# A gated graph network block on one Trainium2 core: first states normalised from a transposed input, with another order of calls

## The chip, the cores and the metric

One core of one Trainium2 chip runs the whole kernel. The metric is the device time in microseconds of that core.

## The reference, cut to what matters

There are 16 graphs of 512 nodes with 128 features each (`x`), and a 512x512 0/1 matrix per graph (`adj`). Two residual layers follow each other.

```
h = relu(layernorm(x))
for i in 0, 1, 2:                        # gated graph network
    m = h @ weight[i];  aggr = A^T @ m
    h = gru(aggr, h)                     # r, z = sigmoid, n = tanh, h = (1-z) n + z h
x = x + h
h = relu(layernorm(x))                   # graph attention, one head
p = h @ W.T;  e = leaky_relu(p@a1 + (p@a2)^T);  mask e where adj == 0
x = x + softmax(e) @ p
```

All values are float32. The normalisations run along the 128 features of a node, with a mean, a variance and eps = 1e-5.

## The kernel before, in words

Nodes of a graph are tiled as C = 4 chunks of P = 128. A "natural" tile has the nodes of a chunk on the partitions and the features along the row (128 x 4 x 128). A "turned" tile has the 128 features on the partitions and the 512 nodes along the row. The GRU works on turned states `hT[s]`; the product with the adjacency takes natural states as weights. A float32 operand of these products is split in a high part (fp32r) and the rest, the low part: `nat_hi`, `nat_lo`, `hT_hi`, `hT_lo`, `agg_hi`, `agg_lo`. A product with a split weight and a split operand is three matmuls of 512 columns (`three`, L1196 to L1198).

**Stages.** Iteration i is a software pipeline over graphs. It does GRU step 0 of graph i, step 1 of graph i-1, step 2 of graph i-2, the second normalisation and projection of graph i-3 (`GA`), and the attention of graph i-4 (`GB`). The steps inside an iteration go 2, 1, 0. Each engine has its own list of calls, written out by hand: `full(i)` for iterations 5 to 15, single lines for the first and the last ones. Waits are on semaphores inside the helpers, so an engine never goes past a call that waits. The order of calls on PE (matmul), DVE, ACT, POOL and the SP queue is therefore the order of the work.

**The first state.** POOL makes from mean and variance (DVE, `x_stats` L693, `x_mean` L702) the scale and the offset of each node: `norm_scale`, L248 to L254, four operations on 128x4. ACT makes `h0 = relu(x*scale + offset)` in natural form (`normed`, L349, four operations of 128x128). PE turns `h0` with four transposes into the PSUM bank `X` (`turn_input`, L1252). ACT copies the bank twice, as `hT[0]` (`first_state`, L362) and as its high part (`first_state_high`, L367). The low part is made on DVE (L742), the natural high part on DVE (`natural_high0`, L728), the natural low part on POOL (`natural_low0`, L260).

**The second normalisation.** DVE makes statistics of `x2` (L815, L822). POOL subtracts the mean (`centre2`, L275), makes the scale (`scale2`, L282 and L284) and multiplies (`normed2`, L291), both on 128x512. PE turns the result (`turn_normed`, L1282), ACT applies relu (`attention_input`, L429), PE projects (`project`, L1298), ACT copies the projection (`values`, L436 and L437).

**The attention.** PE spreads a column over the partitions (`neighbour_terms`, L1306). DVE adds the mask and takes the maximum (`scores`, L838, four of 128x512) and makes the exponents' offsets with four operations of 128x4 (`offsets`, L849, L851, L854, L855). ACT makes two exponentials per chunk (`exps`, L448 and L449), DVE their maximum (`probabilities`, L862). PE turns a chunk (`turn_prob`, L1323), ACT copies it (`turned_prob`, L455), PE multiplies (`attend`, L1338). DVE writes the output (`output`, L881), SP stores it.

**A GRU step.** PE: `neighbours` (L1212, eight matmuls), `from_state` and `from_neighbours` for the banks HN, R, Z and IN. ACT: `neighbours_high` L385, `own_candidate` L395, `reset_gate` L405, `update_gate` L415, `candidate` L423. DVE: `neighbours_low` L754, `reset` L763, `before_tanh` L773, `keep` L781, `renew` L789, `new_state` L799. Then `state_high` (L373 on ACT), `state_low` (POOL L269 or DVE L742), `turn_state` (L1262), `natural_high` (L379) and `natural_low` (L748); the last state goes through `turn_result` (L1273) and `residual` (L807).

**Loads.** The SP queue issues for each graph `x` (256 KB), the adjacency (1024 KB), and later the store. `load_x(i)` waits for `residual` of graph i-4; a ring of four holds the inputs.

Of the kernel before, what the change touches and what calls it, by code (L numbers as in the profile page):

```python
# [27 lines left out]
P = 128  # L28
# [6 lines left out]
def graph_block(nc, x, adj, inner, outer, out):  # L35
# [4 lines left out]
    GA, GB = LAYERS, LAYERS + 1  # L40
    ITERATIONS = B + GB
# [27 lines left out]
    with ExitStack() as ctx:  # L69
# [34 lines left out]
        rstd1 = sb("rstd1", [P, C])  # L104
        mr1 = sb("mr1", [P, C])
        off1 = sb("off1", [P, C])
# [25 lines left out]
        x2c = sb("x2c", [P, C, D])  # L132
        h2n = sb("h2n", [P, C, D])
        h2T = sb("h2T", [P, N])
        hp = sb("hp", [P, RING, C, D + 2])
# [11 lines left out]
        probT = sb("probT", [P, C, C, P])  # L147
# [34 lines left out]
        hT0_done = sem("hT0_done")  # L182

        g_turned, x2_done, st2_done, mv2_done = (sem(n) for n in ("g_turned", "x2_done", "st2_done", "mv2_done"))
        eps2_done, rstd2_done, x2c_done, h2n_done = (sem(n) for n in ("eps2_done", "rstd2_done", "x2c_done", "h2n_done"))
# [9 lines left out]
        def _(sp):  # L195
# [39 lines left out]
        def _(pool):  # L235
# [6 lines left out]
            def norm_scale(i, k):  # L242

                if on(i, 0):
                    pool.wait_ge(mv1_done, (i + 1) * C)
                    if i > 0:
                        pool.wait_ge(h0_done, i * C)
                    pool.tensor_scalar(ve1[:], mv1[:, :, 1], EPS, 0.25, ALU.add, ALU.mult).then_inc(eps1_done, 1)  # L248
                    pool.wait_ge(eps1_done, i + 1)
                    pool.tensor_tensor(rstd1[:], ve1[:], halves[:], ALU.pow).then_inc(rstd1_done, 1)  # L250
                    pool.wait_ge(rstd1_done, i + 1)
                    pool.tensor_tensor(mr1[:], mv1[:, :, 0], rstd1[:], ALU.mult).then_inc(mr1_done, 1)
                    pool.wait_ge(mr1_done, i + 1)
                    pool.tensor_scalar(off1[:], mr1[:], -1.0, None, ALU.mult).then_inc(off1_done, 1)  # L254
# [16 lines left out]
            def centre2(i, k):  # L271

                if on(i, GA) and not last_step(i) and not gru_done(i):
                    pool.wait_ge(mv2_done, (i - (GA - 1)) * C)
                    pool.tensor_tensor(x2c[:], x2[:, i % 3], mv2[:, :, 0:1].broadcast_to([P, C, D]),  # L275
                                       ALU.subtract).then_inc(x2c_done, 1)

# [7 lines left out]

            def normed2(i, k):

                if on(i, GA) and not last_step(i) and not gru_done(i):
                    pool.wait_ge(x2c_done, i - (GA - 1))
                    pool.wait_ge(rstd2_done, i - (GA - 1))  # L290
                    pool.tensor_tensor(h2n[:], x2c[:], rstd2[:].rearrange("p (c o) -> p c o", o=1).broadcast_to([P, C, D]),  # L291
                                       ALU.mult).then_inc(h2n_done, 1)
# [11 lines left out]
            norm_scale(1, 1)  # L304
            norm_scale(2, 2)
            natural_low0(1, 1)
            state_low(1, 1, 2)
            state_low(1, 1, 1)
            natural_low0(2, 2)
            state_low(2, 2, 2)  # L310
            norm_scale(3, 3)
            state_low(2, 2, 1)
            scale2(3, 3)
            natural_low0(3, 3)
            centre2(3, 3)
            normed2(3, 3)
            norm_scale(4, 0)
            state_low(3, 3, 2)
            state_low(3, 3, 1)
            natural_low0(4, 0)  # L320

            for i in range(5, 16):
# [3 lines left out]
            centre2(15, 3)  # L326
            scale2(15, 3)
            normed2(15, 3)
            state_low(15, 3, 1)
            scale2(16, 0)  # L330
            centre2(16, 0)
            normed2(16, 0)
# [1271 lines left out]
```

## Time and profile before

| | |
|---|---|
| median of 3 runs | 466.82 us (466.74 to 468.75) |
| profiled execution, its own time | 466.79 us |
| its span in the profile | 464.9 us |
| granted TensorE clock, mean | 0.999 |
| busy: PE, DVE, ACT, POOL | 97%, 91%, 76%, 32% of the span |
| DMA | 26.42 MB, mean 57 GB/s |

The span is what the engines' records cover, and 1.9 us of the profiled execution's own time lie around it. A busy share is the union of the records of an engine. Records of one engine overlap: a matmul of 512 columns has a record of about 0.39 us, while the next starts 0.23 us after it, and a DVE operation of 0.68 us is followed by the next after 0.60 us. Where work is counted below, it is counted from start to start.

### The profile page before, as it was taken

Reading aid. Unit: us, or ns where it says so; the run is one execution under the profiler, and the core shown is the slowest. Engines: PE = TensorE matmul, PEld = TensorE weight load, DVE = VectorE, ACT = ScalarE, POOL = GpSimd, SP = SyncE. Lnnn points to the kernel's source line nnn. Section 1 sums busy time; section 2 is a strip of 40 time slices with the busy share of each in tenths; the row PEclk is TensorE's granted clock in tenths of the full one; section 3 lists DMA queues with packets and bytes.
Section 4 is the critical chain, followed back from the end, with each engine's and each line's share of the span. In section 5 each row is a group of like instructions: output and inputs, shape, how many; then the busy total and the mean of one; then the engine's idle time right before and its main releaser. Section 6 shows DMA issues by size and latency. Waiting matters only on the chain.

```text
span 464.9 us, 8212 instructions
## 1 busy us (share of the span) xinstructions
PE 451.0 (97%) x2616; PEld 383.0 (82%) x2616; DVE 424.6 (91%) x1101; ACT 351.7 (76%) x636; POOL 147.7 (32%) x165
## 2 busy tenths in 40 slices
PE   8999999999999999999999999999999999998886
PEld 7778778888888888888888888888888888887675
DVE  4979978999999999999999999999999998988986
ACT  3485667878879787877978787896878789595693
POOL 3134163233424224332422423241342324131110
PEclk9999999999999999999999999999999999999999
DMA  8220210200203020020303011030301100000001
GB/s 335 90 90 2 62 52 1 113 10 20 111 24 113 25 113 25 22 93 24 113 25 115 23 35 80 24 115 23 114 23 60 55 25 1 23 2 23 2 23 47
DMA packets 7242, 26.42 MB, mean 57 GB/s; under 512 B 800, under 2 KB 800, under 8 KB 5152
## 3 DMA queue, kind: packets, MB, share of 16 engines
q1 hardware_dynamic: 7200, 25.90, 15.0%
q8 instruction: 22, 0.36, 0.3%
q14 instruction: 20, 0.16, 0.1%
HBM read 21.70 MB, written 4.19 MB: 56 GB/s over the span
## 4 chain that ended last, share of the span: by engine, by line
PE 79%; DVE 6%; issue 5%; ACT 5%; POOL 2%; DMA 1%; POOLq 0%; DVEq 0%; ACTq 0%
PE X L1212 16%; PE G L1338 8%; PE G L1323 5%; PE Z L1196 4%; PE R L1196 4%; PE Z L1198 4%; PE Z L1197 4%; PE R L1198 4%; PE R L1197 4%; PE X L1262 3%; PE G L1298 2%; PE HN L1198 2%; PE HN L1196 2%; PE HN L1197 2%; PE IN L1196 2%
## 5 line engine op out<-in xcount | busy, mean ns | idle before, releaser
L1212 PE MATMUL X<-A_ring,nat_hi 128*128 128x512 f32 x192 | 78.2, 407 | 0.0
L1212 PE MATMUL X<-A_ring,nat_lo 128*128 128x512 f32 x192 | 75.4, 393 | 0.0
L1338 PEld LDWEIGHTS G<-hp,probT 128*128 128x128 f32 x480 | 60.0, 191 | 4.9 <-ACT probT L455 1.8
L1338 PE MATMUL G<-hp,probT 128*128 128x128 f32 x480 | 61.3, 275 | 1.3 <-ACT probT L455 1.3
L405 ACT ACTIVATE tr<-R,bias 128x512 f32<-128x512 f32 x48 | 33.4, 695 | 26.1 <-PE R L1198 25.9
L269 POOL TENSOR_TENSOR hT_lo<-hT,hT_hi 128x512 fp32r<-128x512 f32 x19 | 25.4, 1339 | 79.1 <-ACT hT_hi L373 58.8
L448 ACT ACTIVATE e<-g,nb 128x512 f32<-128x512 f32 x64 | 46.5, 726 | 4.2 <-DVE nb L855 3.0
L455 ACT COPY probT<-G 128x512 f32<-128x512 f32 x60 | 35.5, 592 | 16.8 <-PE G L1323 15.2
L862 DVE SCALAR_TENSOR_TENSOR prob<-e 128x512 f32<-128x512 f32 x64 | 44.6, 699 | 4.0 <-ACT e L449 3.7
L449 ACT ACTIVATE e<-g,nb 128x512 f32<-128x512 f32 x64 | 45.9, 717 | 0.0
L1212 PEld LDWEIGHTS X<-A_ring,nat_hi 128*128 128x128 f32 x192 | 36.0, 188 | 8.5 <-DVE nat_lo L748 0.9
L1212 PEld LDWEIGHTS X<-A_ring,nat_lo 128*128 128x128 f32 x192 | 36.1, 188 | 6.9
L415 ACT ACTIVATE tz<-Z,bias 128x512 f32<-128x512 f32 x48 | 33.0, 688 | 10.4 <-PE Z L1198 10.2
L838 DVE CUSTOM_DVE_ANT_0 g<-G,neg_ring 128x512 f32<-128x512 f32 x60 | 37.8, 687 | 3.3 <-PE G L1306 3.3
L423 ACT ACTIVATE gn<-npre,outer_in 128x512 f32<-128x512 f32 x48 | 35.2, 733 | 4.5 <-DVE npre L773 4.2
L1323 PE MATMUL G<-ident,prob 128*128 128x128 f32 x240 | 36.3, 274 | 1.9 <-DVE prob L862 1.1
L385 ACT CAST agg_hi<-X 128x512 fp32r<-128x512 f32 x48 | 27.9, 581 | 13.5 <-PE X L1212 13.5
L754 DVE TENSOR_TENSOR agg_lo<-X,agg_hi 128x512 fp32r<-128x512 f32 x48 | 32.8, 684 | 5.6 <-ACT agg_hi L385 5.6
L763 DVE SCALAR_TENSOR_TENSOR rv<-tr,hnb 128x512 f32<-128x512 f32 x48 | 33.9, 707 | 2.9 <-ACT tr L405 2.5
L260 POOL TENSOR_TENSOR nat_lo<-h,nat_hi 128x512 fp32r<-128x512 f32 x15 | 20.4, 1357 | 50.6 <-DVE nat_hi L728 50.6
L789 DVE SCALAR_TENSOR_TENSOR fresh<-tz,gn 128x512 f32<-128x512 f32 x48 | 33.0, 687 | 3.6 <-ACT gn L423 1.7
L799 DVE SCALAR_TENSOR_TENSOR hT<-kept,fresh 128x512 f32<-128x512 f32 x48 | 33.1, 690 | 2.6 <-DVE kept L781 0.9
(144 smaller groups left out, 1220.5 us busy)
## 6 DMA issues: line engine op xcount, KB each, us to landing
adj_raw<-in_adj SPq DMA_DIRECT2D x16, 1024.0 KB, 4.9
x_ring<-in_x SPq DMA_DIRECT2D x16, 256.0 KB, 2.7
out_x<-out_sb SPq DMA_DIRECT2D x8, 256.0 KB, 2.0
out_x<-inner_in SPq DMA_DIRECT2D x8, 256.0 KB, 2.0
inner_in<-in_inner SPq DMA_DIRECT2D x1, 384.0 KB, 5.7
outer_in<-in_outer SPq DMA_DIRECT2D x1, 325.0 KB, 5.2
```

The source lines that it names most:

```text
L423: act.activation(gn[:], npre[:], ACT.Tanh, bias=vecs[:, 2:3]).then_inc(gn_done, 1)
L448: act.activation(e1[:, c % 2], g[:, k % 2, c], ACT.Exp, bias=nb1[:, k % 2, c:c + 1])
L449: act.activation(e2[:, c % 2], g[:, k % 2, c], ACT.Exp, bias=nb2[:, k % 2, c:c + 1], scale=SLOPE).then_inc(exp_done, 1)
L455: act.copy(probT[:, c], G1[:]).then_inc(probT_done, 1)
L838: dve.tensor_tensor_reduce(out=g[:, k % 2, c], in0=(HN if gru_done(i - 1) else G0)[:], in1=neg_ring[:, k, c], scale=1.0, scalar=-3.0e38, o ...
L862: dve.scalar_tensor_tensor(out=prob[:, c], in0=e1[:, c % 2], scalar=1.0, in1=e2[:, c % 2], op0=ALU.mult, op1=ALU.max, accum_out=psums[:, k ...
L1196: pe.matmul(acc[:], w_lo, v_hi, start=start, stop=False)
L1197: pe.matmul(acc[:], w_hi, v_lo, start=False, stop=False)
L1198: return pe.matmul(acc[:], w_hi, v_hi, start=False, stop=stop)
L1212: mm = pe.matmul(X[:], part[s][:, c], A_ring[:, (k - s) % RING, c], start=(c == 0 and part is nat_hi), stop=(c == C - 1 and part is nat_lo))
L1323: mm = pe.transpose(own[:, j * P:(j + 1) * P], prob[:, c, j * P:(j + 1) * P], ident[:])
L1338: mm = pe.matmul(own[:, c * D:(c + 1) * D], probT[:, c, j], hp[:, (k + 3) % RING, j, 0:D], start=(j == 0), stop=(j == C - 1))
```

## The change

1. `x` also comes turned from the host, as `xT` (16, 128, 512). For graphs 3 to 15 (`FIRST = 3`) there is no `turn_input` on PE.
2. SP stores scale and offset of such a graph (128 x 8 numbers) to a DRAM scratch and loads them back, spread over all partitions (`norm_rows`, two DMAs, the second waits for the first on the queue), and loads `xT[i]` (`load_xT`).
3. POOL multiplies and adds in place (`scale_turned`, `shift_turned`, two operations of 128x512, whose second input has a step of 8 numbers). ACT makes `hT[0]` and its high part from the result with a relu.
4. The second normalisation becomes one scale and one offset per node: POOL makes them (two more operations of 128x4), ACT applies them (`normed2`, four operations of 128x128). `centre2` and the multiplication on POOL are gone, for all graphs but the last two, where DVE does it as before.
5. `hp` and `probT` have rings of three in place of four. Buffers only, no work.
6. All lists of calls are in another order.

```diff
+            def load_xT(i):
+                if i > FIRST:
+                    sp.wait_ge(hT0_done, i)
+                    sp.wait_ge(hi_done[0], i)
+                sp.dma_start(x_turned[:], xT[i]).then_inc(xT_loaded, 16)
+            def norm_rows(i):
+                sp.wait_ge(off1_done, i + 1)
+                if i > FIRST:
+                    sp.wait_ge(rows_loaded, (i - FIRST) * 16)
+                sp.dma_start(columns[i % 2].rearrange("(p f) -> p f", p=P), norm1[:].rearrange("p a c -> p (a c)")).then_inc(columns_stored, 16)
+                sp.wait_ge(columns_stored, (i - FIRST + 1) * 16)
+                if i > FIRST:
+                    sp.wait_ge(shifted_done, i - FIRST)
+                sp.dma_start(rows[:].rearrange("q p a c -> q (p a c)"), columns[i % 2].partition_broadcast(P)).then_inc(rows_loaded, 16)
...
                 if on(i, 0):
                     load_x(i, i % RING)
                     load_adjacency(i, i % RING)
+                    if i >= FIRST:
+                        norm_rows(i)
+                        load_xT(i)
...
+            def scale_turned(i, k):
+                    pool.tensor_tensor(x_turned..., x_turned..., rows[:, :, 0].rearrange("q p c -> q c p"), ALU.mult).then_inc(scaled_done, 1)
+            def shift_turned(i, k):
+                    pool.wait_ge(scaled_done, i - FIRST + 1)
+                    pool.tensor_tensor(x_turned..., x_turned..., rows[:, :, 1].rearrange("q p c -> q c p"), ALU.add).then_inc(shifted_done, 1)
...
# POOL, full(i)
-                centre2(i - 1, (i - 1) % RING)
+                scale_turned(i - 1, (i - 1) % RING)
+                shift_turned(i - 1, (i - 1) % RING)
+                natural_low0(i - 1, (i - 1) % RING)
                 scale2(i - 1, (i - 1) % RING)
-                normed2(i - 1, (i - 1) % RING)
                 norm_scale(i, i % RING)
                 state_low(i - 1, (i - 1) % RING, 1)
-                natural_low0(i, i % RING)
...
# ACT, full(i), as it is after the change
natural_high(i-1, 2); state_high(i-1, 2); update_gate(i-1, 0); values(i-1); candidate(i-1, 0)
neighbours_high(i, 2); state_high(i-1, 1); normed(i); reset_gate(i, 2); own_candidate(i, 2)
natural_high(i, 1); exps(i, 0); update_gate(i, 2); first_state(i); exps(i, 1)
neighbours_high(i, 1); turned_prob(i, 0); first_state_high(i); own_candidate(i, 1); exps(i, 2)
turned_prob(i, 1); exps(i, 3); reset_gate(i, 1); candidate(i, 2); turned_prob(i, 2)
update_gate(i, 1); neighbours_high(i, 0); normed2(i); candidate(i, 1); turned_prob(i, 3)
reset_gate(i, 0); attention_input(i); own_candidate(i, 0)
# DVE, full(i), as it is after the change
keep(i-1, 0); state_low(i-1, 2); renew(i-1, 0); new_state(i-1, 0); neighbours_low(i, 2)
scores(i); offsets(i); natural_low(i, 1); residual(i); probabilities(i, 0); reset(i, 2)
x2_stats(i); natural_high0(i); probabilities(i, 1); neighbours_low(i, 1); before_tanh(i, 2)
keep(i, 2); state_low(i, 0); probabilities(i, 2); x_stats(i+1); x2_mean(i); adjacency(i)
reset(i, 1); renew(i, 2); probabilities(i, 3); x_mean(i+1); new_state(i, 2); before_tanh(i, 1)
neighbours_low(i, 0); mask(i); keep(i, 1); renew(i, 1); new_state(i, 1); output(i)
reset(i, 0); natural_low(i, 2); before_tanh(i, 0)
# PE, full(i), as it is after the change
neighbours(i, 2); neighbour_terms(i); from_state(2, HN); from_state(2, R); from_neighbours(2, R)
turn_state(i, 1); from_state(2, Z); from_neighbours(2, Z); from_state(1, R); turn_result(i)
from_neighbours(2, IN); neighbours(i, 1); turn_prob(0); from_state(1, HN); from_state(1, Z)
turn_prob(1); attend(0); from_neighbours(1, IN); from_neighbours(1, R); turn_prob(2); attend(1)
from_neighbours(1, Z); from_state(0, R); neighbours(i, 0); attend(2); from_state(0, Z)
turn_prob(3); from_neighbours(0, R); from_state(0, HN); turn_normed(i); attend(3)
turn_state(i, 2); from_neighbours(0, Z); from_neighbours(0, IN); project(i)
```

In iterations 16 and 17 the GRU calls come earlier in the lists of PE, ACT and DVE, ahead of part of the attention of graphs 12 and 13: on PE `from_neighbours(16, 1, R)` and `(16, 1, IN)` now stand ahead of `attend(16, 0)` (the IN one stood behind `attend(16, 3)`), and on DVE `natural_low(16, 2)` now stands ahead of `scores(17)` and `neighbours_low(17, 2)` ahead of `residual(17)`.

## Rows read from the trace of the kernel before

**Rows 1.** Busy time by stretch, one iteration: us, busy PE, PEld, DVE, ACT, POOL, clock, DMA.

```profile
104.10:131.00 26.90, 26.90 (x160) 23.13 (x159) 25.75 (x68) 21.93 (x40) 9.23 (x10) 1.00 0.16 60
```

**Rows 2.** The chain that ended last: `project` of iterations 4 and 11 (start us, us).

```profile
104.35 0.89 PE G L1298 x8
...
292.50 0.89 PE G L1298 x8
```

**Rows 3.** Timeline of PE: a block of four transposes between 512-column matmuls (start, us).

```profile
189.00 0.60 PE L1306 MATMUL G<-ident,hp 128*128 128x128 f32 x4
189.36 0.48 PE L1196 MATMUL HN<-hT_hi,whh_lo 128*128 128x512 f32 x1
189.67 0.39 PE L1197 MATMUL HN<-hT_lo,whh_hi 128*128 128x512 f32 x1
```

**Rows 4.** Groups by line, PE `turn_input`: xcount, busy us, mean ns, idle before.

```profile
L1252 PE MATMUL X<-ident,h 128*128 128x128 f32 x64 | 9.7, 273 | 1.0 <-ACT h L349 0.6 <-DVE agg_lo L754 0.3
```

**Rows 5.** Timeline of PE: `turn_input` of graph 3 and the wait before it.

```profile
67.65 0.63 PE L1252 MATMUL X<-ident,h 128*128 128x128 f32 x4 [0.27 <-DVE agg_lo L754]
```

**Rows 6.** Timeline of ACT in the iteration that begins at 185.68 us.

```profile
185.95 0.48 ACT L436 COPY hp<-G 128x390 f32<-128x390 f32 x1 [0.20 <-PE G L1298]
...
186.49 0.74 ACT L423 ACTIVATE gn<-npre,outer_in 128x512 f32<-128x512 f32 x1
...
189.86 0.61 ACT L373 CAST hT_hi<-hT 128x512 fp32r<-128x512 f32 x1
...
192.87 0.72 ACT L448 ACTIVATE e<-g,nb 128x512 f32<-128x512 f32 x1
...
194.12 0.67 ACT L415 ACTIVATE tz<-Z,bias 128x512 f32<-128x512 f32 x1
194.69 0.71 ACT L448 ACTIVATE e<-g,nb 128x512 f32<-128x512 f32 x1
...
195.91 0.56 ACT L385 CAST agg_hi<-X 128x512 fp32r<-128x512 f32 x1
```

**Rows 7.** Timeline of DVE in the same iteration: `new_state`, first `scores`, first and last of `offsets`.

```profile
188.06 0.69 DVE L799 SCALAR_TENSOR_TENSOR hT<-kept,fresh 128x512 f32<-128x512 f32 x1
...
189.64 0.69 DVE L838 CUSTOM_DVE_ANT_0 g<-G,neg_ring 128x512 f32<-128x512 f32 x1 [0.28 <-PE G L1306]
...
192.21 0.16 DVE L849 TENSOR_TENSOR top<-hp,gmax 128x4 f32<-128x4 f32 x1
...
192.68 0.15 DVE L855 SCALAR_TENSOR_TENSOR nb<-hp,ltop 128x4 f32<-128x4 f32 x1
```

**Rows 8.** Timeline of POOL in the same iteration: `norm_scale` begins and ends, `state_low`.

```profile
185.14 0.19 POOL L248 TENSOR_SCALAR ve<-mv 128x4 f32<-128x4 f32 x1 [6.02 <-DVE mv L702]
...
186.97 0.55 POOL L254 TENSOR_SCALAR off<-mr 128x4 f32<-128x4 f32 x1
190.55 1.30 POOL L269 TENSOR_TENSOR hT_lo<-hT,hT_hi 128x512 fp32r<-128x512 f32 x1 [3.04 <-ACT hT_hi L373]
```

**Rows 9.** DMA issues by line: xcount, KB each, median us to landing.

```profile
x_ring<-in_x SPq DMA_DIRECT2D x16, 256.0 KB, 2.7
```

**Rows 10.** Groups by line, ACT `normed`: xcount, busy us, mean ns, idle before.

```profile
L349 ACT ACTIVATE h<-x_ring,off,rstd 128x128 f32<-128x128 f32 x64 | 26.4, 486 | 7.0 <-POOL off L254 7.0
```

**Rows 11.** Timelines of POOL and DVE: the two places where DVE operations are unusually long.

```profile
42.94 2.20 POOL L260 TENSOR_TENSOR nat_lo<-h,nat_hi 128x512 fp32r<-128x512 f32 x1 [0.37 <-DVE nat_hi L728]
...
43.91 1.78 DVE L763 SCALAR_TENSOR_TENSOR rv<-tr,hnb 128x512 f32<-128x512 f32 x1
...
415.81 1.04 POOL L291 TENSOR_TENSOR h2n<-x2c,rstd 128x512 f32<-128x512 f32 x1
...
415.82 1.57 DVE L862 SCALAR_TENSOR_TENSOR prob<-e 128x512 f32<-128x512 f32 x1 [0.79 <-ACT e L449]
```

**Rows 12.** Timeline of DVE at the end: `new_state` of graph 15, steps 1 and 2.

```profile
423.82 0.69 DVE L799 SCALAR_TENSOR_TENSOR hT<-kept,fresh 128x512 f32<-128x512 f32 x1
...
436.95 0.69 DVE L799 SCALAR_TENSOR_TENSOR hT<-kept,fresh 128x512 f32<-128x512 f32 x1
```

More of the change, by code:

```diff
@@ L40, in graph_block @@
     GA, GB = LAYERS, LAYERS + 1
+    FIRST = 3
     ITERATIONS = B + GB
@@ L319, in _ @@
             state_low(3, 3, 1)
+            scale_turned(4, 0)
+            shift_turned(4, 0)
             natural_low0(4, 0)
-            for i in range(5, 16):
+            scale2(4, 0)
+            norm_scale(5, 1)
+            state_low(4, 0, 1)
+            for i in range(6, 16):
                 full(i)
-            centre2(15, 3)
+            scale_turned(15, 3)
+            shift_turned(15, 3)
+            natural_low0(15, 3)
             scale2(15, 3)
-            normed2(15, 3)
             state_low(15, 3, 1)
             scale2(16, 0)
-            centre2(16, 0)
-            normed2(16, 0)
             state_low(16, 0, 2)
@@ L423, in candidate, with normed2 @@
                     act.activation(gn[:], npre[:], ACT.Tanh, bias=vecs[:, 2:3]).then_inc(gn_done, 1)
+            def normed2(i, k):
+                if on(i, GA) and not last_step(i) and not gru_done(i):
+                    act.wait_ge(off2_done, i - (GA - 1))
+                    for c in range(C):
+                        nd = act.activation(h2n[:, c], x2[:, i % 3, c], ACT.Identity, bias=off2[:, c:c + 1], scale=rstd2[:, c:c + 1])
+                    nd.then_inc(h2n_done, 1)
             def attention_input(i, k):
@@ L551, in _ @@
             reset_gate(3, 3, 1)
+            normed2(3, 3)
             update_gate(3, 3, 1)
@@ L946, in _ @@
             state_high(0, 0, 1)
-            x_mean(2, 2)
             state_low(0, 0, 1)
             natural_low(1, 1, 1)
+            x_stats(2, 2)
+            x_mean(2, 2)
             adjacency(1, 1)
-            adjacency(2, 2)
+            wi_low(1)
             neighbours_low(1, 1, 1)
-            wi_low(1)
+            x_stats(3, 3)
+            mask(2, 2)
             reset(1, 1, 1)
@@ L1055, in _ @@
             reset(4, 0, 0)
-            x_mean(5, 1)
             natural_low(4, 0, 2)
@@ L1108, in _ @@
             probabilities(16, 0, 0)
+            before_tanh(16, 0, 2)
+            probabilities(16, 0, 1)
+            keep(16, 0, 2)
+            neighbours_low(16, 0, 1)
             residual(16, 0)
+            renew(16, 0, 2)
+            probabilities(16, 0, 2)
+            new_state(16, 0, 2)
             x2_stats(16, 0)
-            keep(16, 0, 2)
             x2_mean(16, 0)
-            probabilities(16, 0, 1)
-            probabilities(16, 0, 2)
-            before_tanh(16, 0, 2)
-            neighbours_low(16, 0, 1)
+            reset(16, 0, 1)
             probabilities(16, 0, 3)
-            renew(16, 0, 2)
-            reset(16, 0, 1)
-            new_state(16, 0, 2)
-            output(16, 0)
             before_tanh(16, 0, 1)
@@ L1125, in _ @@
             new_state(16, 0, 1)
+            output(16, 0)
+            natural_low(16, 0, 2)
             scores(17, 1, 0, 4)
             offsets(17, 1, 0, 4)
-            natural_low(16, 0, 2)
+            neighbours_low(17, 1, 2)
             residual(17, 1)
@@ L1132, in _ @@
             probabilities(17, 1, 0)
+            reset(17, 1, 2)
             probabilities(17, 1, 1)
-            neighbours_low(17, 1, 2)
+            before_tanh(17, 1, 2)
             normed2(17, 1)
-            probabilities(17, 1, 2)
-            reset(17, 1, 2)
-            before_tanh(17, 1, 2)
             keep(17, 1, 2)
@@ L1141, in _ @@
             new_state(17, 1, 2)
-            scores(18, 2, 0, 4)
+            probabilities(17, 1, 2)
+            probabilities(17, 1, 3)
             residual(18, 2)
-            offsets(18, 2, 0, 4)
             x2_stats(18, 2)
             x2_mean(18, 2)
-            probabilities(17, 1, 3)
+            scores(18, 2, 0, 4)
+            offsets(18, 2, 0, 4)
+            normed2(18, 2)
             probabilities(18, 2, 0)
-            normed2(18, 2)
             probabilities(18, 2, 1)
@@ L1494, in _ @@
             from_neighbours(4, 0, 0, IN)
-            turn_state(4, 0, 2)
-            for i in range(5, 16):
+            project(4, 0)
+            for i in range(5, 15):
                 full(i)
-            from_state(15, 3, 0, Z)
+            neighbours(15, 3, 2)
+            neighbour_terms(15, 3)
+            from_state(15, 3, 2, HN)
+            from_state(15, 3, 2, R)
+            from_neighbours(15, 3, 2, R)
+            turn_state(15, 3, 1)
+            from_state(15, 3, 2, Z)
+            from_neighbours(15, 3, 2, Z)
@@ new lines, in _ @@
+            from_state(15, 3, 1, R)
+            turn_result(15, 3)
+            from_neighbours(15, 3, 2, IN)
+            neighbours(15, 3, 1)
+            turn_prob(15, 3, 0)
+            from_state(15, 3, 1, HN)
+            from_state(15, 3, 1, Z)
+            turn_prob(15, 3, 1)
+            attend(15, 3, 0)
+            from_neighbours(15, 3, 1, IN)
+            from_neighbours(15, 3, 1, R)
+            turn_prob(15, 3, 2)
+            attend(15, 3, 1)
+            from_neighbours(15, 3, 1, Z)
```

497 lines of the change are left out of this document (262 added, 235 removed).

## The prediction
> **What bounds the kernel now.** First I read the busy time by stretch: in a full iteration PE is busy for all of its 26.90 us, DVE for 25.75, ACT for 21.93 [rows 1]. Then the chain of waits gives the period: `project` starts at 104.35 and, seven iterations on, at 292.50, so one iteration takes 188.15 / 7 = 26.88 us [rows 2]. The timeline of PE shows no gap inside it. So each microsecond taken from PE in the twelve full iterations 4 to 15 is gained, as far as DVE and ACT keep up. Outside them, up to graph 3 and after iteration 15, chains of single operations count as well. I measure the change against the profiled execution, 466.79 us of its own time; the median of the runs, 466.82, is the same number. A difference of 0.5% (2.3 us) is about what a measurement of this kernel can tell from no change.
>
> **PE turns removed.** `turn_input` runs 16 times with four transposes, 64 instructions [rows 4]; 13 of these calls go, 12 of them in the full iterations. The mean of 273 ns is a record's length, not its price. From start to start, a block of four transposes takes 189.36 - 189.00 = 0.36 us, and the first matmul behind it 189.67 - 189.36 = 0.31 us where one matmul behind another takes 0.23, so entering a block costs 0.08 more [rows 3]. Before, `turn_input` stands next to a `turn_prob` and shares that 0.08; but the new list of PE has ten changes of kind per iteration where the old one has eleven. That is 0.36 + 0.08 = 0.44 per iteration. Laying out the new PE list call by call with these prices gives a period of 26.45 us; the same prices laid on the old list give 26.88. Twelve iterations: 12 x 0.43 = 5.2 us. In graph 3 the turn had also waited 0.27 us for `agg_lo` [rows 5], and a wait may stay: between 0.4 and 0.8, I take 0.6.
>
> **The spread by DMA.** `norm_rows` needs scale and offset. `norm_scale` takes 186.97 + 0.55 - 185.14 = 2.4 us [rows 8] and now follows `x_mean`, which the new DVE list places some 18.5 us into the iteration before; behind `scale2` and waits for DVE it ends near 22. Two DMAs in a row follow, and `xT` behind them. No small store and no spread load is in the trace; the nearest row is the load of `x`, 2.7 us for 256 KB [rows 9]. At 2.7 each plus 0.4 to issue, the rows are there 2 us into the iteration, and POOL asks for them no earlier than 5.1, behind `state_low`. The cover is 3 us: the two DMAs may cost 9 in place of 6 before anything moves. Queued behind them on SP are the store, which nothing waits for soon, and `load_x(i+1)`, which waits for `residual` some 8 us into the iteration anyway. Cost nothing; if the cover is gone, `first_state` comes late by the excess.
>
> **POOL.** It loses `centre2` and `normed2` and gains two operations of the same 128x512, 1.04 us each [rows 11], plus two of 128x4. It is busy 9.23 of 26.90 us [rows 1], so this is hidden. What a second input with a step of 8 numbers costs is not in the trace. Between 1.04 us, the row of the same shape, and twice that, I take 1.04, the nearest row, with the other end in the rivals.
>
> **ACT.** `normed2` adds four operations of 128x128: the mean of `normed` is 486 ns [rows 10], some 0.39 from start to start, 1.6 us per iteration, in front of `candidate(i, 1)`. That makes `renew(i, 1)` ready at about 22.1 us in my layout, where DVE, after `mask` and `keep(i, 1)`, arrives at 22.1. So no one waits. `first_state` and `first_state_high` are two ACT operations as before. ACT goes from 21.9 to 23.5 busy of 26.45.
>
> **The second loop.** The new order leaves little slack on one path. After `project` come `values` (0.27 later), `candidate` (0.8 later) [rows 6], `renew`, `new_state` at about n = 2.3, `neighbours_low`, four `scores`, `offsets`. `offsets` ends 192.68 + 0.15 - 188.06 = 4.8 us after `new_state` before [rows 7], of which 0.4 was waiting for `neighbour_terms`, which stands earlier now: 4.4. Then ACT runs without a pause until the third pair of exponentials: three pairs of 1.25 (192.87 to 194.12) and six single operations between 0.47 and 0.57 (194.12 to 194.69) [rows 6], together 6.9, then `probabilities`, 0.8. So `turn_prob(2)` can start at 2.3 + 4.4 + 6.9 + 0.8 = 14.4 to 14.5; PE gets there at 14.5. The two loops are equal, and I give 0.06 per iteration, 0.7 us, for it (bounds 0 and 2).
>
> **Ends.** Until graph 3 the chain is as before: 0, within 1 either way. In the last iterations the GRU of graph 15 is brought forward; its `new_state` started at 423.82 and 436.95 [rows 12]. Laid out by hand, the first comes some 4 us sooner and the second some 2.4, but the attention pushed back has to be done by DVE in the same stretch. Bounds: 1 lost, 3.5 gained; I take 1.5 gained.
>
> Sum: 466.8 - 5.2 - 0.6 + 0.7 - 1.5 = **460.2 us**.
>
> **Rival A: `shift_turned` holds up `offsets`.** This is the one that ends slower. Rows show the mechanism: `reset` took 1.78 us and `probabilities` 1.57 us where they take 0.68 elsewhere, both while a POOL operation of 128x512 ran; the second started 0.01 us after POOL's and got through 0.14 before its end (415.82 + 1.57 - 0.68 = 416.71, against 416.85) [rows 11]. Both read two tiles from SBUF. The Trainium skill (SBUF — State Buffer, "Who interferes with whom") says that a DVE instruction with two SBUF inputs contends with a GpSimd instruction that reads SBUF and that the later one waits for the whole of the other; the two places agree. In the new order, counted from the start of `new_state`: it takes 0.72 with its hand-over, the cast on ACT 0.61, `state_low` 1.30 [rows 6, 8], three hand-overs 0.25, `scale_turned` 1.04, so `shift_turned` runs from 3.93 to 4.97. `offsets` would run from 0.6 + 0.6 + 2.57 = 3.8 to 4.4 [rows 7], and its operations read `hp`, `gmax` and `top`, two SBUF inputs each. If the first slips through and the next is held, the exponentials start 0.66 to 0.86 later, and by the second loop the whole iteration does: 27.1 to 27.3 us against 26.88, so 12 x 0.2 to 12 x 0.4 = 2.6 to 5 us more than before, less 2.1 for graph 3 and the end: 467.3 to 469.7, middle 468.5. It decides from a delay of 0.6 us per iteration on: above that the kernel is slower than before. Against it: two is all that the trace has of DVE held by POOL, no operation of 128x4 among them, and my layout would have to be right to 0.3 us. No run here shows what an operation of four numbers does.
>
> **Rival B: the stepped input is slow on POOL.** At 1.5 us in place of 1.04, `shift_turned` ends about 5.9 after `new_state`, `offsets` is held for 1.6, the period is 28.1, and the sum 466.8 + 12 x 1.2 - 2.1 = 479. For it speaks only that the step is new; for the first value, that POOL's operations here are bound by more than reading, since the same shape takes 1.04 with a broadcast input and 1.30 with an fp32r output [rows 8, 11]. The Trainium skill (Advanced Engine Details and Errata, "SBUF Cachelines") says that accesses which each touch another 16-byte line are penalised; a step of 32 bytes is of this kind, and no run here shows what it costs POOL.
>
> **Rival C: the gain is waited away.** ACT with 23.5 of 26.45 us and DVE with 25.7 have less room, some call comes late by a few tenths, and the period stays near 26.8: 466.8 - 1 - 2.1 = 463.7, between 462 and 466. For it: DVE has only 0.7 us left. Against it: DVE's records overlap, and from start to start it needs about 25.4.
>
> **Rival D: the spread comes late**, so the part does not do what it says and `first_state` waits for a DMA. It needs 9 us for two DMAs. With 10 us it would be 1 late, 0.5 of it felt: 466.8 + 0.6 - 2.1 = 465.3.
>
> **How the numbers follow.** The forecast (PE-bound, 458 to 462) has 0.45, A 0.30, B 0.07, C 0.13, D 0.05. The likeliest is 460.2. The range takes in the forecast, C, D and all of A, and leaves out B and the far ends: 457.5 to 470.5. Faster by over 0.5% (below 464.5): the forecast with its bounds 0.44, most of C 0.08, giving 0.52. Slower (above 469.1): a third of A 0.10, B 0.07, a little of D 0.02, giving 0.19. The rest, 0.29, is within 0.5%.
>
> **What would show it.** Right: `project` every 26.4 to 26.5 us, no wait of PE over 0.1 in the full iterations, no `turn_input` after graph 2, the spread rows landed before POOL's `state_low` ends, the last `new_state` over 2 us nearer to the start than the period alone explains. A: operations of `offsets` with records of 0.8 to 1.0 us in place of 0.16, `turn_prob(2)` waiting for `prob`, a period above 27. B: records of `scale_turned` and `shift_turned` of 1.5 us or more. C: PE waits spread over several lines. D: POOL idle before `scale_turned`, released by a DMA. A period above 26.88 would make the forecast wrong.

## The result: 482.6 us in place of 466.6

The changed kernel takes 482.62 us (median of 6 runs, 482.41 to 484.22), the kernel before 466.63 (6 runs, 464.89 to 468.75). The ratio is 1.0348, with a 95% interval of 1.0322 to 1.0374: slower by 3.5%. The forecast was 460.2, its range ended at 470.5.

The profiled execution of the changed kernel has a span of 482.4 us, that of the kernel before 464.9. It is the slowest of the six (484.22 us); the spans therefore differ by 17.5 us where the medians differ by 16.0. To see where the 17.5 us arose, cut both spans at the start of `neighbours(4, 2)` and of `neighbours(16, 2)` on the timeline of PE (before: 77.93 and 401.42; after: 78.21 and 418.50). Twelve iterations lie between the cuts.

| part of the span | before | after | difference | forecast |
|---|---|---|---|---|
| up to `neighbours(4, 2)` | 77.9 | 78.2 | +0.3 | -0.6 |
| 12 iterations | 12 x 26.96 | 12 x 28.36 | +16.8 | -4.5 |
| from `neighbours(16, 2)` | 63.5 | 63.9 | +0.4 | -1.5 |

The last row holds 1.3 us of a fall of TensorE's clock in this one execution, told at the end. The iterations are the loss. The page of the changed kernel (busy time; the shares of the chain that ended last; two groups with their idle time and its releaser):

```profile
PE 456.2 (95%) x2564; PEld 375.5 (78%) x2564; DVE 444.0 (92%) x1101; ACT 370.7 (77%) x692; POOL 182.1 (38%) x191
...
PE 44%; DVE 26%; ACT 20%; issue 8%; POOL 1%; DVEq 0%; POOLq 0%; ACTq 0%
...
L1268 PE MATMUL X<-A_ring,nat_hi 128*128 128x512 f32 x192 | 78.8, 410 | 10.3 <-DVE nat_lo L804 10.2
...
L500 ACT ACTIVATE e<-g,nb 128x512 f32<-128x512 f32 x64 | 46.2, 722 | 20.7 <-DVE nb L911 20.6
```

The chain now runs through DVE and ACT for nearly half of the span, and the exponentials waited 20.6 us for `nb`, the last result of `offsets`, in 12 iterations: 1.7 us each. The timeline of one iteration, from `new_state` on, answers to [rows 7, 8] (start, us, engine, line, operation, idle before). `top`, `ltop` and `nb` are the tiles that the four operations of `offsets` write:

```profile
194.09 0.69 DVE L855 SCALAR_TENSOR_TENSOR hT<-kept,fresh 128x512 f32<-128x512 f32 x1
...
195.51 1.29 POOL L313 TENSOR_TENSOR hT_lo<-hT,hT_hi 128x512 fp32r<-128x512 f32 x1 [7.88 <-ACT hT_hi L417]
...
196.76 1.72 POOL L292 TENSOR_TENSOR x_turned<-x_turned,rows 128x512 f32<-128x512 f32 x1
...
197.85 0.65 DVE L905 TENSOR_TENSOR top<-hp,gmax 128x4 f32<-128x4 f32 x1
...
198.54 0.16 DVE L907 SCALAR_TENSOR_TENSOR ltop<-top 128x4 f32<-128x4 f32 x1
198.56 1.61 POOL L298 TENSOR_TENSOR x_turned<-x_turned,rows 128x512 f32<-128x512 f32 x1
198.74 1.46 DVE L910 TENSOR_TENSOR nb<-hp,ltop 128x4 f32<-128x4 f32 x1
...
200.12 0.15 DVE L911 SCALAR_TENSOR_TENSOR nb<-hp,ltop 128x4 f32<-128x4 f32 x1
200.19 0.68 DVE L804 TENSOR_TENSOR nat_lo<-X,nat_hi 128x512 fp32r<-128x512 f32 x1
200.30 0.72 ACT L500 ACTIVATE e<-g,nb 128x512 f32<-128x512 f32 x1 [1.70 <-DVE nb L911]
...
200.93 0.50 PE L1268 MATMUL X<-A_ring,nat_hi 128*128 128x512 f32 x1 [0.86 <-DVE nat_lo L804]
```

`top`, four numbers per partition, takes 0.65 us in place of 0.16 and ends when `scale_turned` ends (198.50 against 198.48). `nb` takes 1.46 and ends with `shift_turned` (200.20 against 200.17). The iteration shown is like the others: over all thirteen of each the medians are 0.64 and 1.45. So `offsets` is over 6.18 us behind `new_state` (200.12 + 0.15 - 194.09), where I had laid out 4.4. Both POOL operations last 1.6 to 1.7 us where I had 1.04. The mechanism of rival A and the price of rival B came together, and each made the other worse.

The spread arrived in time: the record of `scale_turned` shows no wait for a DMA. For the next iteration `rows` was issued at 217.44 and takes 4.3 us to land (median), `xT` at 218.22 and 4.4; the iteration begins at 220.07, so they are there 1.7 and 2.6 us into it, and `scale_turned` asks at 5.05.

### The profile page after: what moved, and what is told of

Same layout as the page of the kernel before. It is cut to its first block, busy times and chain, and to the rows that moved or that the text cites. A ratio compares the mean times of both kernels' runs of the same rounds, so it can differ in the third digit from the quotient of the medians.

```text
span 482.4 us, 8251 instructions
## 1 busy us (share of the span) xinstructions
PE 456.2 (95%) x2564; PEld 375.5 (78%) x2564; DVE 444.0 (92%) x1101; ACT 370.7 (77%) x692; POOL 182.1 (38%) x191
## 4 chain that ended last, share of the span: by engine, by line
PE 44%; DVE 26%; ACT 20%; issue 8%; POOL 1%; DVEq 0%; POOLq 0%; ACTq 0%
PE G L1394 8%; PE X L1268 8%; DVE g L894 7%; ACT e L501 4%; PE G L1379 4%; ACT e L500 4%; DVE nb L910 4%; ACT tz L459 3%; PE R L1252 2%; PE R L1253 2%; PE R L1254 2%; PE Z L1252 2%; DVE agg_lo L810 2%; PE Z L1254 2%; PE Z L1253 2%
## 5 line engine op out<-in xcount | busy, mean ns | idle before, releaser
L1394 PE MATMUL G<-hp,probT 128*128 128x128 f32 x480 | 63.9, 277 | 0.0
L500 ACT ACTIVATE e<-g,nb 128x512 f32<-128x512 f32 x64 | 46.2, 722 | 20.7 <-DVE nb L911 20.6
L304 POOL TENSOR_TENSOR nat_lo<-h,nat_hi 128x512 fp32r<-128x512 f32 x15 | 24.1, 1606 | 55.1 <-DVE nat_hi L784 50.6
L1379 PEld LDWEIGHTS G<-ident,prob 128*128 128x128 f32 x240 | 27.9, 142 | 19.8 <-DVE prob L918 14.7
L1379 PE MATMUL G<-ident,prob 128*128 128x128 f32 x240 | 37.6, 280 | 5.4 <-ACT probT L507 3.4
L319 POOL TENSOR_SCALAR ve<-mv 128x4 f32<-128x4 f32 x16 | 14.9, 929 | 64.8 <-DVE mv L878 64.7
L439 ACT ACTIVATE hnb<-HN,bias 128x512 f32<-128x512 f32 x48 | 32.7, 681 | 3.7 <-PE HN L1254 2.1
## 6 DMA issues: line engine op xcount, KB each, us to landing
inner_in<-in_inner SPq DMA_DIRECT2D x1, 384.0 KB, 5.9
```

Of the source, the lines that this page charges most:

```text
L500: act.activation(e1[:, c % 2], g[:, k % 2, c], ACT.Exp, bias=nb1[:, k % 2, c:c + 1])
L1379: mm = pe.transpose(own[:, j * P:(j + 1) * P], prob[:, c, j * P:(j + 1) * P], ident[:])
L1394: mm = pe.matmul(own[:, c * D:(c + 1) * D], probT[:, (i * C + c) % 3, j], hp[:, (i - 1) % 3, j, 0:D], start=(j == 0), stop=(j == C - 1))
```

## The experiments

Every run stands beside runs of the kernel before that were measured together with it; their medians lie between 466.67 and 466.98 us. Periods come from the first and last start of a POOL operation over ten iterations where such a row exists; this is the row of `shift_turned` (durations in ns, first and last start) in the changed kernel and in the run *small*:

```profile
L298 POOL TENSOR_TENSOR x_turned<-x_turned,rows x11: 1578/1608/1617, 113.5 to 397.0; 128x512 f32<-128x512 f32 x11
```

```profile
L298 POOL TENSOR_TENSOR x_turned<-x_turned,rows x11: 198/199/200, 108.8 to 374.8; 128x4 f32<-128x4 f32 x11
```

(397.0 - 113.5) / 10 = 28.35 and (374.8 - 108.8) / 10 = 26.60.

| run | us | ratio [95%] | period |
|---|---|---|---|
| changed kernel | 482.62 | 1.0348 [1.0322, 1.0374] | 28.35 |
| small | 460.44 | 0.9878 [0.9843, 0.9913] | 26.60 |
| flat | 473.42 | 1.0175 [1.0110, 1.0239] | 27.63 |
| behind | 468.66 | 1.0042 [1.0025, 1.0059] | 27.11 |
| flat_behind | 462.77 | 0.9920 [0.9891, 0.9949] | 26.66 |
| alone | 474.62 | 1.017 [1.0146, 1.0195] | 27.61 |
| alone_behind | 471.74 | 1.0097 [1.0075, 1.0119] | 27.37 |
| real_behind | 521.41 | 1.1175 [1.1146, 1.1204] | 31.51 |
| early | 473.83 | 1.0136 [1.0086, 1.0185] | 27.42 |
| node_order | 476.75 | 1.0204 [1.0184, 1.0225] | 27.76 |
| shift_only | 471.27 | 1.009 [1.0073, 1.0107] | 27.37 |
| quarters | 482.35 | 1.0333 [1.0298, 1.0369] | 28.45 |
| quarters_behind | 471.11 | 1.0101 [1.0077, 1.0124] | 27.35 |

**small.** Both operations on 4 columns; everything else of the change stays, the DMAs and waits too.

```
- pool.tensor_tensor(<x_turned, 128x512>, <x_turned>, <rows, stepped>, ...)
+ pool.tensor_tensor(x_turned[:, 0:C], x_turned[:, 0:C], rows[:, 0, 0], ALU.mult)   # and rows[:, 0, 1], ALU.add
```

> The changed kernel with the two POOL operations on x_turned (multiply, add) cut from 128x512 to 128x4 numbers; the first states of graphs 3 to 15 are then not normalised. All else, the loads and the waits too, is as in the changed kernel. Theory (POOL's two long operations hold the port on which DVE's offsets read): offsets back to some 0.16 us per operation, period 26.4 to 26.5 us in place of 28.36, so 482.6 - 12 x 1.9 = 459.8 us. Rival (the DMA spread, the ACT load of normed2 or the new order of calls costs the time): the period stays above 27.5, over 472 us.

It hit: 460.44 us, with a period of 26.60 where 26.4 to 26.5 was expected. Without the two operations the kernel is what I had forecast (460.2), so the spread, `normed2` on ACT and the new order together cost little that I had not counted. `offsets` is fast again on the timeline of DVE:

```profile
185.59 0.69 DVE L855 SCALAR_TENSOR_TENSOR hT<-kept,fresh 128x512 f32<-128x512 f32 x1
...
189.36 0.16 DVE L905 TENSOR_TENSOR top<-hp,gmax 128x4 f32<-128x4 f32 x1
189.56 0.16 DVE L907 SCALAR_TENSOR_TENSOR ltop<-top 128x4 f32<-128x4 f32 x1
189.75 0.16 DVE L910 TENSOR_TENSOR nb<-hp,ltop 128x4 f32<-128x4 f32 x1
189.83 0.15 DVE L911 SCALAR_TENSOR_TENSOR nb<-hp,ltop 128x4 f32<-128x4 f32 x1
```

With `new_state` at 185.59, offsets ends at 189.83 + 0.15 = 189.98, 4.39 behind it (I had 4.4). The changed kernel's offsets ends 6.18 - 4.39 = 1.79 later, and its period is 28.35 - 26.60 = 1.75 longer: what offsets loses, the iteration loses, nearly one for one.

**flat.** The second input contiguous: 512 neighbouring numbers of `rows`, which are other numbers than the scale and the shift.

```
- rows[:, :, 0].rearrange("q p c -> q c p")
+ rows[:].rearrange("q p a c -> q (p a c)")[:, 0:N]      # shift: [:, N:2 * N]
```

> The changed kernel with the second input of the two POOL operations read in one piece (the first and the last 512 of the 1024 spread numbers) in place of a step of 8; so it multiplies and adds the wrong numbers. Tells the price of the step from the price of the collision. Theory: the records of the two operations fall from 1.72 and 1.61 to some 1.04 us, offsets is still held, but by 0.66 to 0.86 in place of 1.8 us: period 27.1 to 27.3, 467 to 470 us. Rival (the step alone is the cause, without it there is no collision): period 26.5, 460 us. Rival (the time of a POOL operation does not depend on the step): no change, 482.6 us.

Slower than expected, at 473.42. The timelines of POOL and DVE:

```profile
193.06 1.30 POOL L292 TENSOR_TENSOR x_turned<-x_turned,rows 128x512 f32<-128x512 f32 x1
...
194.14 0.23 DVE L905 TENSOR_TENSOR top<-hp,gmax 128x4 f32<-128x4 f32 x1
...
194.43 1.29 POOL L298 TENSOR_TENSOR x_turned<-x_turned,rows 128x512 f32<-128x512 f32 x1
194.60 1.14 DVE L910 TENSOR_TENSOR nb<-hp,ltop 128x4 f32<-128x4 f32 x1
```

A multiplication or addition of two contiguous tiles takes POOL 1.30 us, not the 1.04 that I took from the row with a broadcast input [rows 11]. The stepped input adds 0.4 to it (1.70 in *shift_only* below, where nothing else is on it). So two errors lay in my price, and the larger part of the miss, 13.2 of 22.4 us, is there even without the step: `top` is held for 0.07 us only, up to the end of `scale_turned`, and `nb` to the end of `shift_turned`.

**behind.** Numbers and step as in the change, but the second operation waits for `offsets` (`nb_done` counts its last two operations, `GB` is 4):

```
  pool.wait_ge(scaled_done, i - FIRST + 1)
+ if i >= GB:
+     pool.wait_ge(nb_done, (i - (GB - 1)) * 2)
```

> The changed kernel with one more wait: shift_turned of graph i waits until the offsets of the same iteration are done. Right numbers. Theory: scale_turned still holds the first operation of offsets by some 0.5 us, but the second no longer holds the third by 1.3: the exponentials start 0.6 late in place of 1.8; shift_turned ends some 6.7 us after new_state, just ahead of first_state. Period 27.1, 467 us. Rival (it is the amount of POOL work, not its place): DVE is held elsewhere instead and the period stays near 28.4, 482 us.

468.66 us where 467 was expected: 14 of the 16 us are gone with one wait. `scale_turned` still holds `top` (0.65 us in place of 0.16), hence a period of 27.11, 0.51 above *small*. `shift_turned`, in its new place, also holds the first `prob` (0.99 us in place of 0.68).

**flat_behind.** Both edits.

> Both edits: second inputs in one piece (so the wrong numbers) and shift_turned behind the offsets. Theory: scale_turned ends about when offsets begins and shift_turned begins behind it, so nothing is held: the same as with operations of 128x4, period 26.4 to 26.6, 459 to 461 us. Rival (two full operations on POOL cost DVE time wherever they stand): period above 26.9, over 465 us.

462.77, a little above what was expected; the period of 26.66 is that of *small* within 0.06. The profiled execution has the fall of the clock at its end; the one execution with a mean granted clock of 0.999 took 461.6.

**shift_only.** `scale_turned` on 4 columns, `shift_turned` whole, in its place.

> The changed kernel with scale_turned on 4 columns only (the first states of graphs 3 to 15 are left unscaled but for these), shift_turned whole and stepped. Theory: shift_turned starts 2.95 us behind new_state and ends at 4.6, the first operation of `offsets` (from 3.8) is held until then, 0.8 us instead of 0.16, the later one not at all: offsets is over 0.7 to 0.8 later than with both cut, period 27.3 to 27.4, 468.5 to 470 us. If the loss came from POOL's total work and not from the place, half of it would be left: period 27.5, 471.5 us; if each operation costs its own holding, whatever its place, 1.3 us an iteration, 476 us.

The period was as the place demands, (384.0 - 110.3) / 10 = 27.37; the time, 471.3, is 1.3 above the expected range. Two executions with a mean granted clock of 1.000 took 470.7, two with 0.996 took 471.9 and 472.0, so the clock explains about half of it. The timelines of POOL and DVE show what rival A had described:

```profile
192.44 1.70 POOL L298 TENSOR_TENSOR x_turned<-x_turned,rows 128x512 f32<-128x512 f32 x1
...
193.23 0.93 DVE L905 TENSOR_TENSOR top<-hp,gmax 128x4 f32<-128x4 f32 x1
```

**alone.** The collision in the kernel before, with nothing of the change: one useless addition on POOL behind `state_low`, in 11 iterations. It writes `x2c`, so `centre2` also waits for it, but begins some 9 us later.

```
  state_low(i - 1, (i - 1) % RING, 1)
+ pool.tensor_tensor(<x2c>, outer_in[:, 0:N], outer_in[:, P:P + N], ALU.add)
```

> The kernel before, unchanged but for one 128x512 addition of two SBUF tiles on POOL right behind state_low, in 11 iterations; nothing reads its result. Theory (a POOL operation under `offsets` is what costs, whatever else the change did): it starts 3.85 us behind new_state, lasts 1.0 to 1.3 us, the first operation of `offsets` (0.16 us, at 4.15) ends with it at about 5.1, all of offsets 0.7 to 0.9 us later, period 26.96 -> 27.7 to 27.8, 474.5 to 476.5 us. Rival (the loss needs the change's other parts, its shorter layout or its DMAs): offsets is held as long but the path has slack for it, 467 to 470 us. Rival (no holding of such small operations): 466.7 us.

474.62, as expected. The timelines of POOL and DVE:

```profile
194.01 1.30 POOL L304 TENSOR_TENSOR x2c<-outer_in 128x512 f32<-128x512 f32 x1
...
194.40 0.93 DVE L854 TENSOR_TENSOR top<-hp,gmax 128x4 f32<-128x4 f32 x1
```

0.76 us more for offsets (5.53 behind `new_state` against 4.77 [rows 7]), 0.65 more in the period. An operation whose result no one uses, on an engine that is busy a third of the time, costs 1.7% of this kernel.

**alone_behind.** The same, behind `offsets`.

> The same added operation, but it first waits for `offsets` of its iteration, so that it starts behind it. Both theories of a collision: 466.7 to 467.3 us, the 4-column operations back at 0.16 us. If POOL's added work itself costs (its queue, its port time against any other DVE operation): as far above as in the run without the wait, 474 us or more.

A miss: 471.74 in place of 467. `offsets` was fast, but the next DVE operation with two SBUF inputs was caught instead:

```profile
194.28 1.29 POOL L305 TENSOR_TENSOR x2c<-outer_in 128x512 f32<-128x512 f32 x1 [1.13 <-DVE nb L861]
...
194.72 1.41 DVE L769 SCALAR_TENSOR_TENSOR rv<-tr,hnb 128x512 f32<-128x512 f32 x1
```

`reset`'s `rv` took 1.41 in place of 0.68 and is itself on the way to the next state. So this move only chose another victim, at 1.0% in place of 1.7%. In *flat_behind* it costs almost nothing because in the new order the two operations that stand there read PSUM and one SBUF tile each (`nat_lo<-X,nat_hi`, `x<-G,x_ring`).

**early.** `scale_turned` ahead of `state_low`, `shift_turned` behind `offsets`.

> The changed kernel, right numbers, stepped inputs kept: scale_turned goes ahead of state_low on POOL (it can run some 2 us before hT_hi is there) and shift_turned behind `offsets`. Theory A (only the place under `offsets` is costly): period as with nothing there, 26.7, 462 to 464 us. Theory B (any DVE operation with two SBUF inputs is held, and new_state and the one ahead of it lie under scale_turned now): new_state ends up to 1 us later, period 27.2 to 27.6, 468 to 473 us.

473.83, which is theory B (468 to 473) and a little more. DVE and POOL held each other:

```profile
190.29 2.46 POOL L292 TENSOR_TENSOR x_turned<-x_turned,rows 128x512 f32<-128x512 f32 x1 [6.00 <-DMA x_turned<-in_xT]
...
191.31 1.99 DVE L857 SCALAR_TENSOR_TENSOR hT<-kept,fresh 128x512 f32<-128x512 f32 x1
```

`new_state` takes 1.99 in place of 0.69. POOL's own operation takes 2.46 in place of 1.70; `hT_lo` and `fresh` of DVE, with two SBUF inputs too, lie under its start, which is the likely reason and was not tested apart. It also had to wait for the load of `xT`, up to 1.35 us behind the start of the iteration (188.94): the 3 us of cover are gone as soon as `scale_turned` asks earlier.

**real_behind.** The spread in the order in which POOL reads it, by an element-wise store, and `shift_turned` behind `offsets`.

```
- columns[i % 2].rearrange("(p f) -> p f", p=P)
+ columns[i % 2].rearrange("(f p) -> p f", p=P)
```

> The changed kernel with the right numbers and no stepped input: scale and shift are stored into columns element by element, so that the spread tile holds 512 scales and then 512 shifts in order, and shift_turned waits for `offsets`. Theory: as the run with contiguous inputs and that wait, 462.8 us, provided that the store of 1024 elements of 4 bytes for each graph lands within the 2 to 3 us that the spread has in hand. Rival: the store takes longer by some us and scale_turned waits for rows; each us beyond the cover delays scale_turned into `offsets` again, 466 to 470 us.

521.41, far beyond the rival. Mean sizes and medians to landing of the store, first here and then in the changed kernel (DMA issues by line):

```profile
columns<-norm SPq DMA_DIRECT2D x13, 4.0 KB, 8.8
```

```profile
columns<-norm SPq DMA_DIRECT2D x13, 4.0 KB, 1.4
```

1024 elements of 4 bytes take 8.8 us where 128 runs of 32 bytes take 1.4, for the same 4 KB. That is 7.4 us against a cover of about 3. In the iteration with `new_state` at 206.81, `scale_turned` waits 3.39 us for the loads, begins at 212.91, and `rv` of DVE then lies under it (1.77 in place of 0.68). PE runs dry too, and its clock falls: the granted clock is 0.95 in the mean over the run (0.996 in the changed kernel), 0.50 between 220 and 224 us, behind a stretch of 4 us in which PE was busy for 1.22. How much of the 521 us is the wait and how much the clock, this run does not separate.

**node_order.** The order changed on the other side: `x_turned` keeps the four blocks' nodes interleaved, so both POOL inputs are contiguous, and ACT reads `x_turned` stepped by 16 bytes in `first_state`; `xT` is handed over in that order. `shift_turned` waits for `offsets`, as in *behind*.

```
+ columns[i % 2].rearrange("(a p c) -> p a c", a=2, p=P)
- act.activation(hT[0][:], x_turned[:], ACT.Relu)
+ act.activation(hT[0][:].rearrange("q (c p) -> q c p", c=C), x_turned[:].rearrange("q (p c) -> q c p", c=C), ACT.Relu)
```

> The changed kernel with the right numbers, both inputs of scale_turned and shift_turned contiguous (x_turned is kept with the four blocks' nodes interleaved, the first state on ACT reads it stepped, columns is stored in runs of 16 bytes) and shift_turned behind `offsets`. Theory: POOL at 1.30 us each, period 26.7, 462 to 464 us as with contiguous wrong inputs and the wait, faster than both kernels. Rivals: the stepped read makes the two ACT operations of the first state slower (0.62 us each now) and ACT holds up `reset gate` and the exps, 465 us or more; or the 256 runs of 16 bytes land later than the 128 of 32 and scale_turned waits for rows, 466 us or more.

476.75: the first rival. The two ACT groups of the first state (busy us, mean ns):

```profile
L413 ACT ACTIVATE hT_hi<-x_turned 128x512 fp32r<-128x512 f32 x13 | 14.9, 1144 | 0.0
L405 ACT ACTIVATE hT<-x_turned 128x512 f32<-128x512 f32 x13 | 14.6, 1124 | 0.0
```

1.12 us and 1.14 in place of 0.62 and 0.64, twice per iteration, and the period is 1.1 longer (27.76 against 26.66). ACT falls behind, and the second `prob` then starts later than before and lands under POOL's `nat_lo`, 1.56 us in place of 0.69; what each of the two costs was not separated. The second rival did not happen: the store in runs of 16 bytes landed in 2.4 us, and `scale_turned` waited for nothing.

**quarters** and **quarters_behind.** Four operations of 128x128 in place of one; in the second for `scale_turned` only, with `shift_turned` whole and behind `offsets`.

```
+ for c in range(C):
+     pool.tensor_tensor(x_turned[:, c * P:(c + 1) * P], x_turned[:, c * P:(c + 1) * P], rows[:, :, 0, c], ALU.mult)
```

> The changed kernel with scale_turned and shift_turned each as four operations of 128x128 (one per block of nodes) in place of one of 128x512, same places, right numbers. Theory (a DVE operation with two SBUF inputs is held until the POOL instruction under way ends, not for the whole of the work): the pieces last 0.5 to 0.6 us, the two subtractions of `offsets` are held 0.2 to 0.5 us each in place of 0.47 and 1.29, and offsets is over 0.4 to 0.9 later than with nothing there; the shift ends about 7.3 us behind new_state, where ACT asks for it at 6.3, so ACT pays up to 1 us: period 27.1 to 27.7, 466.5 to 473 us. Rival (DVE and POOL share time in proportion, or POOL keeps its claim between its own instructions): offsets is held as in the changed kernel, period 28.4, 482 us.

> Only scale_turned in four pieces, shift_turned whole and behind `offsets`, right numbers. Theory: the first operation of offsets is held 0.2 to 0.4 us in place of 0.47; the shift ends 6.8 us behind new_state, half a microsecond after ACT asks for it: period 26.9 to 27.2, 464.5 to 469 us, as the run with the wait alone (468.7) or better. Rival: as in the changed kernel's first subtraction, 0.65 or more, and 470 us.

482.35 and 471.11, near the 482 and 470 of the rivals: little or nothing is gained over whole operations (*quarters_behind*: `top` 0.54 and `ltop` 0.49 in place of the 0.65 and 0.16 of *behind*). The period of 28.45 holds a fall of the clock near 145 us in the profiled execution; over the eight periods behind it, it is 28.3. The timeline of *quarters* (x4 joins the four pieces):

```profile
197.52 2.12 POOL L293 TENSOR_TENSOR x_turned<-x_turned,rows 128x128 f32<-128x128 f32 x4
...
198.61 0.53 DVE L907 TENSOR_TENSOR top<-hp,gmax 128x4 f32<-128x4 f32 x1
...
199.17 1.94 DVE L909 SCALAR_TENSOR_TENSOR ltop<-top 128x4 f32<-128x4 f32 x1
199.60 1.96 POOL L300 TENSOR_TENSOR x_turned<-x_turned,rows 128x128 f32<-128x128 f32 x4
201.15 0.44 DVE L912 TENSOR_TENSOR nb<-hp,ltop 128x4 f32<-128x4 f32 x1
```

`top` got in at the end of a piece (198.61 + 0.53 = 199.14; the pieces end some 0.53 us apart, the third near 199.11), but `ltop`, 0.16 us alone, was kept out over the last piece of `scale_turned` and about three of `shift_turned`. DVE is not let in at each boundary. What decides it was not tried.

I found no version that computes the whole and beats the kernel before: the best of them, *behind*, is 0.4% slower. *small* and *flat_behind* show what could be had, 0.8 to 1.2%, if both inputs could be contiguous at no cost elsewhere.

## Why the prediction was wrong, point by point

- **PE turns removed** (0.43 per iteration, 26.88 to 26.45): about right. Only the net of this and of the second loop was measured, forecast as 0.37: between the same cuts the twelve iterations take 323.5 us before and 319.4 in *small*, 0.34 each.
- **The spread by DMA** (nothing): right in its effect. The single prices were off in both directions: 1.4 us for the store and 4.3 for the spread, in place of 2.7 each; the sum, 5.7 plus the issues, is near the 5.4 that I had.
- **POOL** (1.04 us each, hidden): this is the step that failed. Measured: 1.72 and 1.61. Of the 0.65 missing, 0.26 is that the row I took had a broadcast input (a plain one is 1.30, *flat*), 0.4 the stepped one (1.70). The row with two plain inputs, `state_low` at 1.30 [rows 8], stood beside it, and I put its length down to the fp32r output; *alone* writes float32 and takes 1.30 too. The range "1.04 to twice" held the measured price; the choice of the nearest row did not. And "hidden" was argued from POOL's busy time, which is beside the point: what counts is which DVE operation starts under it. In place of nothing, the two operations cost 1.75 us per iteration (*small*).
- **ACT** (no one waits for `normed2`): right, as far as *small* shows.
- **The second loop** (0.06 per iteration): close, with nothing holding `offsets` (26.60 against 26.51), and right that it has no slack: 1.79 us on `offsets` made 1.75 us of period.
- **Rival A** (0.30): its mechanism happened, at the operation it named. At 1.04 us each it would, by my layout, have been held once, for 0.66 to 0.86 (no run has POOL operations of that length there); with the measured lengths it was held twice, 0.49 and 1.30. *alone* shows the mechanism by itself. The Trainium skill (SBUF — State Buffer, "Who interferes with whom") says that such a DVE instruction fully waits for the GpSimd one; `top` and `nb`, ending within 0.03 us of POOL's ends, agree, down to four numbers per partition, and so does `scores`, which reads PSUM and one SBUF tile and keeps its 0.68 us under `scale_turned`.
- **Rival B** (0.07): its records (over 1.5 us) were there, and its sum, 479, was the nearest of all. The Trainium skill (Advanced Engine Details and Errata, "SBUF Cachelines") names a penalty for accesses that each touch another 16-byte line, without a size. On POOL it was 0.4 us on 1.30 here, at 32 bytes from one number to the next, and on ACT 0.5 on 0.62 at 16 bytes (*node_order*).
- Treating A and B as alternatives was the second error: a longer POOL operation is the same collision for longer, so the chance of a time above 470 was the chance that POOL takes more than 1.04 us, for whatever reason. Even with the plain price of 1.30 the time is 473.4 (*flat*), outside my range. I gave all of this 0.07, on the word of the nearest row.
- **Ends** (1.5 gained). The GRU came as laid out: `new_state(16, 1)` 18.5 us behind `neighbours(16, 2)`, before 22.4; the second 34.4 against 35.5, 1.1 sooner where I had 2.4. In *small* 0.9 us is gained. In the profiled execution of the changed kernel 0.4 is lost, by the clock, see below. At the start `mask` on DVE was held under `shift_turned` of graph 3, 2.10 us in place of the 1.22 of *small*; *small* reaches `neighbours(4, 2)` at 76.65, the changed kernel at 78.21.

Together, against a span of 464.9: *small* gains 1.3 at the start, 12 x 0.34 = 4.1 and 0.9 at the end, 458.6 in all. The two POOL operations give back 1.6 at the start and 12 x 1.74 = 20.9 in the loop, and the clock takes 1.3 at the end: 482.4.

## What to carry to other kernels

Work moved to a quiet engine is free only if nothing critical needs what it shares. Before putting a POOL operation with SBUF inputs anywhere, list the DVE operations with two SBUF inputs that can start during it, however small, and reckon with each being held to its end; then ask which of them has slack. Price a POOL operation by a row with the same kinds of inputs, plain, broadcast or stepped, and if there is none, let the decision stand on the upper bound.

## What was not expected of the hardware

The clock at the end. Busy time by stretches of 1 us in the changed kernel (columns as in [rows 1]):

```profile
448.50:449.50 1.00, 0.59 (x5) 0.59 (x6) 1.00 (x4) 1.00 (x3) 0.92 (x2) 1.00 0.00 0
449.50:450.50 1.00, 0.77 (x4) 0.29 (x2) 1.00 (x3) 1.00 (x3) 0.86 (x1) 1.00 0.00 0
450.50:451.50 1.00, 0.00 (x0) 0.00 (x0) 1.00 (x5) 1.00 (x3) 0.00 (x0) 0.97 0.00 0
451.50:452.50 1.00, 0.74 (x4) 0.75 (x5) 1.00 (x3) 1.00 (x3) 0.00 (x0) 0.50 0.00 0
452.50:453.50 1.00, 1.00 (x6) 1.00 (x5) 0.97 (x2) 1.00 (x3) 0.00 (x0) 0.50 0.00 0
```

and in *small*, at the same distance from `neighbours(16, 2)`:

```profile
427.02:428.02 1.00, 0.77 (x4) 0.29 (x2) 1.00 (x3) 1.00 (x3) 0.85 (x1) 1.00 0.00 0
428.02:429.02 1.00, 0.00 (x0) 0.00 (x0) 1.00 (x5) 1.00 (x3) 0.00 (x0) 1.00 0.00 0
429.02:430.02 1.00, 0.75 (x6) 0.62 (x7) 1.00 (x3) 1.00 (x3) 0.00 (x0) 1.00 0.00 0
```

PE is busy alike, 0.77 and then 0.00, but in the changed kernel the granted clock falls to half (1.2 GHz) for about 3 us and in *small* it stays at 2.4. The second `new_state` of graph 15 begins 34.43 us behind `neighbours(16, 2)` in both; the last store is issued 61.44 us behind it in place of 60.11, so the fall costs 1.33 us.

It belongs to the execution more than to the kernel. Of the six executions of the changed kernel the two with a mean granted clock of 0.996 took 484.1 and 484.2 us, the four with 0.998 or 0.999 took 482.4 to 482.7; only the first has a trace. *shift_only* has two executions of each kind (see above). The kernel before has executions with 0.995 as well, 468.2 to 468.7 us where those with 0.998 or more take at most 467.1. What decides it in an execution, these runs do not show.

POOL is held by DVE as well, with no wait shown in either queue: the record just gets longer (`scale_turned` 2.46 in *early*; `nat_lo` 1.67 in the changed kernel, where `prob` of DVE lies under its start, and 1.30 in the kernel before). In a trace this reads as a slow operation, and only the other engine's record tells what it is: a held operation of four numbers ends with it (within 0.03 us), a held one of 512 columns some 0.55 us behind it (`new_state` in *early* at 193.30, `scale_turned` at 192.75).
